# Contexts kept transposed, entry operands loaded into rows without a reader, and a reordered fill in a two-layer cross-attention kernel

## The reference, cut to what matters

```
x = x + tanh(g_xattn[0]) * L0_xattn(layernorm(x), ctx_1024, masks)   # self attention, cross attention, feed-forward
x = x + tanh(g_ffn[0])   * L0_ffn(layernorm(x))                      # 8 experts, top 2
x = x + tanh(g_xattn[1]) * L1_xattn(layernorm(x), ctx_1024, mask)    # cross attention with rotary positions
x = x + tanh(g_ffn[1])   * L1_ffn(layernorm(x))                      # 8 experts, top 1
# in both cross attentions, 16 heads of 16:
k = ctx @ Wk + bk ; v = ctx @ Wv + bv ; q = x @ Wq + bq              # L1 rotates q and k by cos/sin tables
out = softmax(q k^T + mask) v @ Wo + bo
```

## Time and profile before

| | us |
|---|---|
| median of 3 runs (lowest, highest) | 1408.83 (1404.21, 1412.75) |
| profiled execution, its own time | 1403.39 |
| its span | 1401.5 |
| PE, DVE, ACT, POOL busy | 1219.7, 769.8, 560.6, 500.7 |

### The profile page before, as it was taken

The page is one execution under the profiler, slowest core; times in us unless marked ns, Lnnn a source line. Parts: engine busy times, 40 slices in busy tenths (PEclk is TensorE's granted clock), DMA queues, the critical chain, the costliest instruction groups (busy, mean ns, idle before and its releaser), DMA issues. The chain is left out here.

```text
span 1401.5 us, 27155 instructions
## 1 busy us (share of the span) xinstructions
PE 1219.7 (87%) x8465; PEld 973.2 (69%) x8520; DVE 769.8 (55%) x2825; ACT 560.6 (40%) x1350; POOL 500.7 (36%) x895
## 2 busy tenths in 40 slices
PE   4699999999998999898999999656687878689996
PEld 3466667777755888788888898533455655589995
DVE  4687777777783487842412121147788876533331
ACT  2265565666665332233333333111354546133331
POOL 3334354454524244420000000256765543433331
PEclk9799999999999999999999999865799999799999
DMA  4776785756520950111111111356364597511110
GB/s 118 163 169 189 198 205 156 162 155 152 145 63 11 356 195 31 42 58 35 36 34 36 34 38 32 85 131 149 99 146 105 85 279 230 180 33 43 41 34 6
DMA packets 126580, 156.16 MB, mean 111 GB/s; under 512 B 19531, under 2 KB 112089, under 8 KB 121564
## 3 DMA queue, kind: packets, MB, share of 16 engines
q1 hardware_dynamic: 116648, 127.14, 35.2%
q0 software_dynamic: 9792, 27.30, 6.3%
HBM read 104.43 MB, written 52.32 MB: 112 GB/s over the span
## 5 line engine op out<-in xcount | busy, mean ns | idle before, releaser
L764 DVE CUSTOM_DVE_ANT_0 att_masked_scores<-att_S,Bm 128x256 bf16<-128x256 f32 x512 | 192.5, 419 | 69.4 <-PE att_S L508 55.4
L645 ACT ACTIVATE att_PT<-att_T 128x512 f32<-128x512 f32 x256 | 151.4, 595 | 93.6 <-PE att_T L527 84.8
L2437 ACT ACTIVATE moe_hT<-moe_H,moe_b 128x128 f32<-128x128 f32 x312 | 89.0, 369 | 194.9 <-PE moe_H L2350 193.6
L2350 PE MATMUL moe_H<-moe_aT,ff_w 128*128 128x128 f32 x1248 | 146.2, 275 | 8.4 <-DVE ff_w L2644 8.4
L2350 PEld LDWEIGHTS moe_H<-moe_aT,ff_w 128*128 128x128 f32 x1248 | 145.1, 192 | 11.7 <-DVE ff_w L2644 9.9
L2362 PE MATMUL moe_Z<-moe_W,moe_hT 128*128 x624 | 142.5, 381 | 0.8 <-DVE moe_z L2651 0.8
L1624 POOL DMA_INDIRECT L_W<-yd,dest x32 | 31.3, 977 | 278.4 <-POOLq L52 269.9
L2362 PEld LDWEIGHTS moe_Z<-moe_W,moe_hT 128*128 128x128 f32 x624 | 115.4, 190 | 15.5 <-issue 1.2
L2651 DVE TENSOR_TENSOR moe_z<-moe_Z,moe_b 128x256 f32<-128x256 f32 x39 | 16.5, 424 | 199.5 <-PE moe_Z L2362 199.5
L508 PE MATMUL att_S<-L_KS,L_QS 96*128 96x256 bf16 x512 | 99.3, 276 | 19.6 <-DMA L_KS<-att_k_dram 14.5
L527 PE MATMUL att_T<-L_QS,L_KS 99*128 99x256 bf16 x512 | 98.7, 273 | 4.8 <-issue 2.3
(11 more groups left out here) (465 smaller groups left out, 2385.5 us busy)
## 6 DMA issues: line engine op xcount, KB each, us to landing
moe_W<-in_L_ffn_W SPq DMA_DIRECT2D x16, 1024.0 KB, 13.7
xd<-zero SPq DMA_DIRECT2D x12, 1280.0 KB
L_W<-in_L_ffn_W POOLq DMA_DIRECT2D x12, 1024.0 KB, 15.3
att_q_dram<-att_pq SPq DMA_DIRECT2D x16, 384.0 KB
att_k_dram<-att_pk SPq DMA_DIRECT2D x16, 384.0 KB
L_QS<-att_q_dram SPq DMA_DIRECT2D x16, 384.0 KB
L_KS<-att_k_dram SPq DMA_DIRECT2D x16, 384.0 KB
moe_xs<-xd SPq DMA_DIRECT2D x39, 128.0 KB
```

The source lines that it names most:

```text
L645: nc.scalar.activation(PT[:, h % 8, :], bankT[h % 2][:, :], ACT.Exp).then_inc(exp_done, 1)
L764: ins = nc.vector.tensor_tensor_reduce(masked_scores[:, h % 2, u, :], bankS[h % 2][:, u * SEQ:(u + 1) * SEQ], masks[m // B][0][:, u * SEQ: ...
L2350: ins = nc.tensor.matmul(bankH[half][:, f * P:(f + 1) * P], w1s[:, cc, g * P:(g + 1) * P], xT[:, s % 2, cc * P:(cc + 1) * P], start=(cc == ...
L2437: ins = nc.scalar.activation(eT[:, s % 2, g * P:(g + 1) * P], bankH[half][:, f * P:(f + 1) * P], ACT.Relu, bias=b1[:, bass.ds(e * NF + g, 1)])
```

## The change

1. In the cross units of layer 0, SP also writes `cT` to a DRAM tensor `turned_ctx` (`keep_context`), 256 KB a unit.
2. In the experts of layer 0, at slot 12, SP issues eight loads of 256 KB (`load_entry`): wk, wv, wq, the key tables cosk and sink, and the transposed contexts 0, 1 and 2. They go to rows of `Y` that nobody reads any more.
3. In layer 1, contexts come transposed. `turn_context` and `bring_context` are gone (8 times 4 transposes and 8 copies), and `load_rotary` issues 10 DMAs where it issued 17. Contexts 3 to 7 are still loaded by `load_rest`, from `turned_ctx`.
4. The fill has another order on every engine, and the normed input goes to a ring of two (`xn`) and not to Y.

```diff
             for b in BEATS:
                 if has(b + 2):
                     stack(b + 2)
+                if has(b + 3) and cross(b + 3):
+                    keep_context(b + 3)
                 if has(b + 3):
                     spread_parts(b + 3, 0)
...
+            def keep_context(m):
+                sp.wait_ge(*taken("c", m))
+                sp.dma_start(turned_ctx[m - B], flat(cT[:, :, :])).then_inc(ctx_kept, 16)
...
                 act.wait_ge(*full("c", m))
+                if m > B:
+                    act.wait_ge(ctx_kept, 16 * (m - B))
                 nc.scalar.activation(flat(cT[:, :, :]), bank_of("c", m)[:, :], ACT.Copy).then_inc(emptied("c", m), 1)
...
-FILL = ("c", 0), ("k", 0), ("v", 0), ("x", 0), ("q", 0), ("c", 1), ("k", 1), ("v", 1), ("x", 1), ("q", 1), ("c", 2), ("k", 2), ("v", 2)
-LAST_FILL = {2: (("x", 2),), 5: (("q", 2),), 9: (("m", 0),), 12: (("x", 3),), 14: (("c", 3),)}
+FILL = ("k", 0), ("v", 0), ("k", 1), ("v", 1), ("x", 0), ("q", 0), ("x", 1), ("q", 1), ("k", 2), ("v", 2)
+LAST_FILL = {2: (("x", 2),), 5: (("q", 2),), 9: (("m", 0),), 12: (("x", 3),)}
...
-    load_context_of(sp, mem, 0)
-    matrix("wk", mem["k_in"])
     columns("bk", mem["k_in"])
-    table("cosk", mem["k_in"])
-    table("sink", mem["k_in"])
-    matrix("wv", mem["v_in"])
     row("bv", mem["v_in"])
     sp.dma_start(mem["mcu"][:, :], ...).then_inc(mem["v_in"], 16)
-    matrix("wq", mem["q_in"])
     columns("bq", mem["q_in"])
     table("cosq", mem["q_in"])
     table("sinq", mem["q_in"])
-    load_context_of(sp, mem, 1)
-    load_context_of(sp, mem, 2)
...
@@ PE @@
-            turn_context(0)
-            keys(0)
-            project_values(0)
-            turn_rows(0)
-            queries(0)
-            turn_context(1)
-            keys(1)
-            project_values(1)
-            turn_rows(1)
-            queries(1)
-            turn_context(2)
+            for m in range(2):
+                keys(m)
+                project_values(m)
+            for m in range(2):
+                turn_rows(m)
+                queries(m)
             keys(2)
             project_values(2)
...
-                    if h == 14 and has(b + 4):
-                        turn_context(b + 4)
...
@@ ACT @@
-            bring_context(0)
+            split(0, 1)
             bring_rows(0)
-            split(0, 1)
-            bring_context(1)
             split(0, 0)
+            first_part(1, 1)
             bring_rows(1)
-            split(1, 1)
-            bring_context(2)
+            second_part(1, 1)
             split(1, 0)
...
@@ POOL @@
             gather(0)
+            parts(0, 1)
+            input_roots(0)
             gather(1)
-            input_roots(0)
-            parts(0, 1)
             parts(0, 0)
             input_roots(1)
+            parts(1, 1)
             gather(2)
-            parts(1, 1)
             parts(1, 0)
...
@@ DVE @@
+            dve.wait_ge(mem["k_in"], 16)
+            turned_keys(0)
+            dve.wait_ge(mem["v_in"], 16 * 2)
+            nc.vector.tensor_copy(mcf[:, :], mem["mcu"][:, :]).then_inc(kept_in, 1)
+            value_rows(0)
             sum_rows(0)
             input_moments(0)
-            dve.wait_ge(mem["k_in"], 16 * 4)
-            turned_keys(0)
+            turned_keys(1)
+            value_rows(1)
             input_norm(0)
-            dve.wait_ge(mem["v_in"], 16 * 3)
-            nc.vector.tensor_copy(mcf[:, :], mem["mcu"][:, :]).then_inc(kept_in, 1)
-            value_rows(0)
+            dve.wait_ge(mem["q_in"], 16 * 3)
+            queries(0)
             sum_rows(1)
             input_moments(1)
-            dve.wait_ge(mem["q_in"], 16 * 4)
-            queries(0)
-            turned_keys(1)
             input_norm(1)
-            value_rows(1)
             queries(1)
             turned_keys(2)
...
+ENTRY_CONTEXTS = 3
+ENTRY = "wk", "wv", "wq", "cosk", "sink"
...
+def load_entry(sp, Y, entry, entered):
+
+    contexts, places = entry_places(Y)
+    for k in ENTRY:
+        sp.dma_start(places[k], entry[k].rearrange("(c p) n -> p c n", p=P)).then_inc(entered, 16)
+    for n in range(ENTRY_CONTEXTS):
+        sp.dma_start(contexts[n], entry["contexts"][n].rearrange("p (c t) -> p c t", c=NC)).then_inc(entered, 16)
...
@@ SP, experts of layer 0 @@
+                if s == EARLY_SLOTS:
+                    sp.wait_ge(r_turned, B)
+                    load_entry(sp, Y, entry, entered)
                 if s + 1 < SLOTS:
                     load(s + 1)
                 if s >= 1:
                     store(s - 1)
```

More of the change, by code:

```diff
@@ L445, in _ @@
             sp.wait_ge(filled0, 16 * (len(fills) + 1))
+            sp.wait_ge(ctx_kept, 16 * B)
         @block.tensor
@@ L875, in rotary_tasks @@
     more = LAST_BEAT.get(h, ()) if b == B - 1 else ()
-    units = [(k, QUADS * b + d if k == "o" else b + d) for k, d in TASKS.get(h, ()) + ROUTE_TASKS.get(h, ())]
+    units = [(k, QUADS * b + d if k == "o" else b + d) for k, d in TASKS.get(h, ()) + ROUTE_TASKS.get(h, ()) if k != "c"]
     last = {"o": QUADS * B, "t": EARLY_SEQUENCES1 - 1, "l": EARLY_SEQUENCES1 - 1, "n": EARLY_SEQUENCES1 - 1}
@@ L903, in rotary_memory @@
     PARTS = 3 * NC * SEQ // 2
-    w = {"wq": by_chunk(part("W2", 1, 0)), "wk": by_chunk(part("W2", 1, 1)), "wv": by_chunk(part("W2", 1, 2)), "wo": sb("wo", [P, NC, D])}
+    contexts, entered = entry_places(Y)
+    w = {"wo": sb("wo", [P, NC, D]), **{k: entered[k] for k in ("wq", "wk", "wv")}}
     w.update({k: sb(k, [P, NC]) for k in ("bq", "bk")})
@@ L907, in rotary_memory @@
     stacks = lambda a: a.rearrange("p (e h t) -> p e h t", e=3, h=H)
-    return {"w": w, "w_in": w_in, "keys": keys, "key_off": key_off, "tables_in": tables, "ctx_in": ctx_in, "stack_rows": stack_rows,
+    return {"w": w, "w_in": w_in, "keys": keys, "key_off": key_off, "tables_in": tables, "ctx_in": turned_ctx, "stack_rows": stack_rows,
             "W1": W1, "W2": W2, "w1s": w1s,
-            "C": [by_chunk(part(("W1", "W2")[m // 4], 0, m % 4)) for m in range(B)],
-            "tables": {k: by_chunk(part("W1", 1, i)) for i, k in enumerate(tables)},
+            "C": contexts + [by_chunk(part(("W1", "W2")[m // 4], 0, m % 4)) for m in range(ENTRY_CONTEXTS, B)],
+            "tables": {"cosk": entered["cosk"], "sink": entered["sink"], **{k: by_chunk(part("W1", 1, i)) for i, k in enumerate(tables)}},
+            "xn": [by_chunk(part("W2", 1, i)) for i in range(2)],
             "fq": part("W2", 1, 3), "fk": part("W1", 2, 0), "rq": part("W1", 2, 1), "rk": part("W1", 2, 2), "tq": part("W1", 2, 3),
-            "tk": part("W2", 2, 0), "cT": by_chunk(part("W2", 2, 1)),
+            "tk": part("W2", 2, 0),
             "pq": three(half["W2", 2][:, 2 * NC * SEQ:2 * NC * SEQ + PARTS]), "pk": three(half["W2", 3][:, 0:PARTS]),
@@ L968, in load_rest @@
     w, w_in = mem["w"], mem["w_in"]
-    for n in range(3, B):
+    for n in range(ENTRY_CONTEXTS, B):
         load_context_of(sp, mem, n)
@@ L1166, in turn_rows @@
                         ins = nc.tensor.transpose(dst[:, cc * SEQ + u * P:cc * SEQ + (u + 1) * P],
-                                                  here(Y, m)[:, u, cc * P:(cc + 1) * P], ident[:, :])
+                                                  xn[m % 2][:, u, cc * P:(cc + 1) * P], ident[:, :])
                 ins.then_inc(filled("x", m), 1)
[L1170 to L1178, removed]
             def product(kind, m, wt, src):
@@ L1195, in keys @@
             def keys(m):
[L1196 to L1199, removed]
+                if m >= ENTRY_CONTEXTS:
+                    pe.wait_ge(mem["c_in"][m], 16)
+                product("k", m, w["wk"], C[m])
             def project_values(m):
-                if m == 0:
-                    pe.wait_ge(mem["v_in"], 16 * 3)
                 pe.wait_ge(*free("v", m))
@@ L1562, in _ @@
                         bring_rows(b + 4)
-                    if h == 14 and has(b + 4):
-                        bring_context(b + 4)
                     quad = QUADS * b + (h - 5) // 4
@@ L1668, in first_expert @@
             def first_expert():
-                pool.wait_ge(*full("c", M - 1))
+                pool.wait_ge(*full("v", M - 1))
                 load_expert(pool, 0)
@@ L1855, in input_norm @@
                 dve.wait_ge(rooted0, n + 1)
-                normal_rows(nc, here(X, n), here(Y, n), t0).then_inc(x_normed, 1)
+                if n >= 2:
+                    dve.wait_ge(*full("x", n - 2))
+                normal_rows(nc, here(X, n), xn[n % 2], t0).then_inc(x_normed, 1)
                 dve.wait_ge(x_normed, n + 1)
@@ L2719, in weights_of @@
                     "gain": a[f"L0_xattn_{norm}_g"], "shift": a[f"L0_xattn_{norm}_b"]}
+        wkv, bkv = a["L1_xattn_Wkv"], a["L1_xattn_bkv"]
+        w = {**{k: a["c_L1_" + k] for k in ("wq", "bq", "wk", "bk")}, "wv": wkv[:, D:2 * D], "bv": bkv[D:2 * D],
+             "wo": a["L1_xattn_Wo"], "bo": a["L1_xattn_bo"]}
         with ExitStack() as f:
@@ L2733, in flamingo @@
```

(2 more changed lines are left out.)

45 lines of the change are left out of this document (18 added, 27 removed).

## The result

| | before | changed |
|---|---|---|
| median, us | 1403.97 (20 runs, 1397.66 to 1412.75) | 1412.89 (20 runs, 1408.02 to 1421.2) |
| profiled execution, us | 1403.39 | 1410.36 |
| its span, us; mean granted clock | 1401.5; 0.945 | 1408.6; 0.941 |

The ratio is 1.0061, with a 95% interval of 1.0048 to 1.0075: slower by 0.6%, 8.6 us of 1404 (6.7 to 10.5). The forecast was 2.3 us faster. The three runs ahead of the prediction had put the kernel before at 1408.83, 4.9 above the median of twenty. So the 1412.9 lies inside the forecast's 1398 to 1413 by luck of the base: as a difference, 8.6 is beyond even its extreme of +6.7.

The account below looks back on a forecast made before the run. Layer 1's fill was taken as bound by latency and written order, layer 0's expert slots by PE with just-in-time loads. +5.9 - 7 - 1.2 = -2.3: 1401.1 us for a profiled-like run, 1406.5 against the median; range 1398 to 1413.

Parts of the forecast that it names:

- Part 1, contexts written out: Layer 0's cross units: eight 256 KB writes and added SP and ACT waits are covered by SP's idle time; cost 0.
- Part 2, the loads at slot 12: Layer 0's experts: loads ahead of slot 13's rows stall PE, net 4.1 plus 1.8 for the clock, 5.9 us.
- streamed at 380 GB/s: 5.5 us: Slot 12: the eight loads' 2.10 MB move at the expert weights' rate, delaying slot 13's rows by 5.5 us.
- the issues ... take 4 us and so don't bind: Slot 12, SP's queue: eight issues of some 0.4 each take less than the transfers' 5.5 us.
- The 0.85: Slot 13: PE's earlier 0.85 us wait for DVE's matrix copy vanishes, reducing the 5.0 us stall to 4.1.
- The clock's 1.8: Slot 13, after PE's stall: work restarts at a lower clock, costing 1.8 us; bounds 0 and 4.1.
- Rival (a): Slot 13's rows are not held back and PE keeps its time: -8.2, 1400.6 us; chance 0.13.
- (b): SP's queue at slot 13 costs more than the fill gives: 11.2 - 7 - 1.2 = +3.0; chance 0.25 shared with another rival.
- The fill, -7: Layer 1's fill: the new order reaches beat 0 earlier by 7 us, the middle of 5.5 and 9; lower bound 4.5.
- 1.8 later: 907.3: Layer 1's fill: gather 0 releases DVE 1.8 us after its last issue ends at 905.5, at 907.3.
- the 4.5 taken and the bound of 7.5: Layer 1's fill: mask bytes land 4.5 us after issue, at 905.6 without a wait; at 7.5 it is 908.6.
- Beats, -1.2: Layer 1's beats: four context turns and copies removed save 0 to 2.4 us, half taken, 1.2.

Follow-up runs that it names:

- loads_alone: The kernel before with nothing but the eight loads at slot 12 added, ahead of slot 13's rows: ratio 1.0041 to the kernel before, 1413.47 us.
- spread_gathers: Changed kernel, eight loads behind slot 13's rows, stack-row loads behind first key parts, gathers 1 and 2 where POOL was idle: 0.9964 of before, 1396.61 us.
- rows_later: The changed kernel with the two stack-row loads issued behind the first write of key parts: ratio 1.0053 to the kernel before, 1412.94 us.
- rows_first: The kernel before with the two stack-row loads at the head of SP's queue instead of its end: ratio 1.0008, 1404.75 us.

## Why the prediction was wrong

It forecast -2.3 and 8.6 came. By the profile's stages (span 7.1 longer): the engines start layer 1 6.4 us later, roots 3 are 1.8 later on top (+80.9 against +79.1), and the rest is 1.2 shorter (420.4 us from roots 3 to the end against 421.6). The 6.4 are slot 13's 8.0 less 1.6, of which this execution was already 1.1 ahead at slot 12's store (681.23 against 682.32).

- **Part 1, contexts written out, cost 0.** Nothing of it shows: the changed kernel reaches the same product before the experts (L2276, 1.14 idle) at 569.75, the kernel before at 570.17.
- **Part 2, the loads at slot 12: mechanism right, size short.** 5.9 forecast, 8.0 in the slot here and 8.0 in loads_alone (5.8 by its ratio). The stall was sized at 5.0 and measured 6.7 over the 0.18 of before. The step that was mis-sized is the rate, "streamed at 380 GB/s: 5.5 us". The window here shows 318 GB/s, and none, four and eight loads ahead give 312. At that rate 2.10 MB take 6.7 us, 1.2 of the 1.7 missing. That "the issues ... take 4 us and so don't bind" is neither refuted nor shown: the eight issues took 4.0 and lay beside the transfers. The 0.85 came back. The clock's 1.8 is 1.9 as measured: (0.69 + 5.31) - (0.44 + 3.65). Rival (a) is out; the queue's price was near the 8.2 from which (b) decides.
- **The fill, -7: this term fell.** It came out as +1.8. The step that failed is the landing of gathers, "1.8 later: 907.3", with its reason that the loads beside gather 0 "are gone". The 1.8 was taken from a gather that travels with little beside it, and the two row loads and two tables were still there. Measured from the end of the last issue, gather 0 took 8.9, gather 2 5.8 and gather 3 1.9. The other steps stand. Keys 0 and values 0 were early. The mask bytes took 5.9 from their issue, between the 4.5 taken and the bound of 7.5, and DVE's wait of 1.22 for them ended long before gather 0 was there. In spread_gathers, where landing is off the path, roots 2 came at +49.7 against the +49.5 written down, and roots 3 5.4 earlier than before. That closeness is in part luck: roots 0 came at +12.4 against the +10.7 of the working, and POOL's list was another.
- **Two causes in the fill.** The first is gather 0 beside the stack-row loads (5.1 us at its sum by rows_later, 2.6 at roots 2). The second is gather 2, which the new order issues behind parts(1, 1) and so beside the stack loads of keys 1; the sum waits 3.37 us for it. The old order, with gather 2 ahead of parts(1, 1), has roots 2 at +55.2 even with the first cause at work. Gather 1 became late only where the row loads had been moved. Mending the first alone gives about the time of before at roots 2. Mending the second by itself in the changed kernel wasn't tried.
- **Beats, -1.2.** From roots 3 to the end, the three profiles with the old layer 1 (before, loads_alone, rows_first) have 421.6, 421.0 and 422.1, and the nine with context turns gone 417.7 to 424.0, with a median of 419.4. That fits 1 to 2 us, but single profiles differ by as much, so it is not shown.
- **The sum** with measured terms: 8.0 + 1.8 - 1.2 = 8.6, by the profiles. That it meets the ratio's 8.6 to the tenth is luck: the -1.2 is not shown, and the two profiles themselves are 7.1 apart. Rival (b), with its sign and +3.0, was the nearest. It gave the slot the blame, where most of the miss was the fill.

What stays open is what delays a gather beside hardware-queue transfers. The Trainium skill (DMA: Bandwidth & Descriptors, "Queues, rings and completion order") says that each DMA engine takes packets from its rings by turns. That would make a gather of small packets wait for a turn behind large ones, but no run here separates this from other reasons, such as the memory or the order of issue.

## What to carry to other kernels

Before a block of prefetches is put into a queue, find the just-in-time load behind it: the same 2.1 MB cost 8 us in that slot ahead of the load, and about half a microsecond in the next one behind it. When a reordering takes loads out of a stage, look at what the freed place lets run together; a landing time read in a quiet stretch doesn't hold beside other transfers. When a slow transfer is moved out of the way, look at who waits for it at its new place. Put a transfer where its issuing engine is idle and well before its use, and check the engine whose work it pushes back.

## What the runs showed of the hardware

- Eight 256 KB loads ahead of a 128 KB one delayed its issue by 4.0 us and lengthened its way from issue to use from 2.1 to 4.8 us; behind it they did neither. In all that is 6.7 us for 2.10 MB, 312 GB/s.
- Behind a wait of PE of 4.08 us the next down products took 4.77 instead of 3.65, with the granted clock at 0.50 when they began. Behind 6.6 to 7.2 us they took between 4.95 and 5.50 in five kernels (5.31 in the changed one).
- Four gather DMAs of 128 KB landed 1.9 us after the end of their issue in a quiet stretch, 5.6 to 6.1 beside three stack loads, and 8.9 beside two loads of 72 KB in three partitions and others. In a window where little else was left, 0.14 of the DMA engines were busy at 18 GB/s; at another place the two took 8.1 us, the same rate.
